# State-space scans: step sizes one operation per slot, no spare decay rows, three taps together, three output pairs on VectorE

## The chip, the core and the metric

The kernel runs on one core of a Trainium2 chip. TensorE (PE), VectorE (DVE), ScalarE (ACT) and GpSimd (POOL) run side by side, each through its own queue in order, and they wait for each other by semaphores; SyncE (SP) issues DMAs. The metric is the time of one execution on the device in microseconds (us), lower is better.

## The reference, cut to what matters

The network has eight blocks on 32 sequences of 113 tokens. The change lies in one of them, the bidirectional state-space block (512 inner channels, 16 states, 4 taps), of which this runs once forward and once on the reversed sequence:

```python
xz = x @ in_w.T
xh, z = jnp.split(xz, 2, axis=-1)
xc = silu(conv_b + sum(xp[:, k:k + L, :] * conv_w[:, k] for k in range(4)))   # xp: xh padded in front
proj = xc @ xproj_w.T                                                        # dt, Bm, Cm
delta = softplus(dt @ dt_w.T + dt_b)
deltaA = exp(delta * A);  deltaBu = (delta * xc) * Bm
h = deltaA * h + deltaBu          # a scan over the tokens, for each of 16 states
y = sum over states of h * Cm;  y = (y + xc * D) * silu(z)
return y @ out_w.T
```

## The kernel before

All tensors keep channels on the 128 partitions; tokens lie along the free axis. The batch is cut into 8 groups of 4 sequences (4 x 113 = 452 columns). A group and a direction make a **half**: 16 halves run in `mamba`, forward and backward in turn, in two calls of `run` of 8 halves each, after a short call that makes the first front. While a half's recurrence runs, the **front** of the half after it (norm, in-projection, convolution, x-projection, step sizes) and the output projection of an earlier one are laid beside it.

The recurrence of a half has 64 **slots**: slot i is state n = i // 4 and channel block j = (0, 2, 1, 3)[i % 4]. In slot i

- ACT computes the decay `dA` = exp(step x A) (`decays`, L1377), into one of two PSUM banks by turns;
- DVE runs the scan (`recur`, L1506) on it and on the input term `dBu`. Blocks 0 and 1 write the state to SBUF (`hs`), blocks 2 and 3 to a PSUM bank (`ssm_ps`); those two DVE multiplies by C itself (`output_term`, L1522);
- POOL makes, once for each state, the output pair of blocks 0 and 1 (`output_terms`, L1462: `hc` = `hs` x C, both in SBUF) and the two input pairs of the next state (`input_terms`, L1451);
- PE adds each `hc` block into the output banks by a product with the identity (`product`, L1286), one slot for each, of the state before.

What else an engine does in a slot stands in its `beside(hf, i)`, by a table of slots at L1137 to L1150: `X_MM` and `Z_MM` (PE in-projections of block m, both into the one bank `XZ`), `TAP` (ACT writes the first tap of the convolution), `CONV` (DVE adds the other three, one in each of the next three slots), `Z_RAW` (ACT copies z out of `XZ`), `SILU` (ACT loads the Silu table, two activations, and loads the Exp table back), `ROWS`, `DT_MM`, `SOFTPLUS` (ACT: Abs, Exp, Ln in one slot), `STEP` (DVE ends the step size). Nothing reorders this: each engine's queue is the order in which the loops write it.

So that the scans can go on while ACT is in a `SILU` slot, ACT computes the decays of the next two slots ahead of it, into `dA_spare` in SBUF (`ahead`, `place`). The scans of these four slots in a half (31, 32, 42, 43) read two SBUF operands, where the others read one from PSUM and one from SBUF.

Of the kernel before, what the change touches and what calls it, by code (L numbers as in the profile page):

```python
# [1117 lines left out]
def mamba(nc, h, c, params):  # L1118
# [18 lines left out]
    MEAN, CENTRE, SQUARE, VAR, RSTD, SCALE = -1, 1, 3, 5, 7, 9  # L1137
    GATE = (2, 3, 5, 6)
    OUT_MM, RES = (8, 11), (10, 13)
    X_MM = [14 + 7 * m for m in range(IB)]  # L1140
    TAP = [16 + 7 * m for m in range(IB)]
    CONV = [15 + 7 * m for m in range(IB)]
    Z_MM = [19 + 7 * m for m in range(IB)]
    Z_RAW = [21 + 7 * m for m in range(IB)]
# [5 lines left out]
    SPARE_ZERO = 50  # L1150

    ahead = {i + 1 + k: 2 + k for i in SILU for k in range(2)}
    place, previous, taken = [], [], {}
    for i in range(SLOTS):
        where = ahead[i] if i in ahead else (i - sum(j < i for j in ahead)) % 2
        place.append(where)
        previous.append(taken.get(where))
        taken[where] = i
    zeroed = {2: -2, 3: -2, place[SLOTS - 2]: -1, place[SLOTS - 1]: 0}
# [3 lines left out]
    with Stage(nc, "ssm_late") as sl, Stage(nc, "ssm") as st:  # L1163
# [93 lines left out]
        def run(parts, weights_late=False):  # L1257
# [8 lines left out]
            with nc.Block(no_gpsimd_drain=True) as block:  # L1266
                @block.sync
                def _(sp):
                    for hf in halves:
# [106 lines left out]
                def _(act):  # L1376
                    def decays(hf, i):  # L1377
                        n, j = i // IB, ORDER[i % IB]
                        if previous[i] is not None:
                            act.wait_ge(s["scan_done"], SLOTS * hf.r + previous[i] + 1)  # L1380
                        elif hf.r:
                            act.wait_ge(s["starts_zero"], 4 * hf.r + zeroed[place[i]])
# [7 lines left out]
                    def beside(hf, i):  # L1390
# [39 lines left out]
                        if hf.front and i in SOFTPLUS:  # L1430
                            m = SOFTPLUS.index(i)
                            at = IB * hf.fronts + m + 1
                            act.wait_ge(s["dt_mm"], at)
# [16 lines left out]
                def _(pool):  # L1450
# [27 lines left out]
                    for k, hf in enumerate(halves):  # L1478
# [3 lines left out]
                        for n in range(S):  # L1482
                            if hf.rec and n:
                                output_terms(hf, n - 1)
# [5 lines left out]
                            if n == S - 3 and hf.front:  # L1490
                                step_input(hf, 0)
                            if n == S - 1:
                                if hf.after:
                                    input_terms(halves[k + 1], 0, 0)
# [1418 lines left out]
```

## Time and profile before

| | us |
|---|---|
| median of 3 runs (lowest, highest) | 6414.39 (6395.42, 6419.84) |
| the profiled execution | 6388.95 |
| its span | 6387.2 |
| of it the 16 halves, about | 1512 to 3341 |

Each number is one profiled execution's. Busy time is of an instruction's own start and end; instructions on DVE overlap by about 0.1 us at their ends, so the step from start to start is what an instruction costs its queue. The idle time of an engine is put down to the instruction that released it.

### The profile page before, as it was taken

Reading aid. Unit: us, or ns where it says so; the run is one execution under the profiler, and the core shown is the slowest. Engines: PE = TensorE matmul, PEld = TensorE weight load, DVE = VectorE, ACT = ScalarE, POOL = GpSimd, SP = SyncE. Lnnn points to the kernel's source line nnn. Section 1 sums busy time; section 2 is a strip of 40 time slices with the busy share of each in tenths; the row PEclk is TensorE's granted clock in tenths of the full one; section 3 lists DMA queues with packets and bytes.
Section 4 is the critical chain, followed back from the end, with each engine's and each line's share of the span. In section 5 each row is a group of like instructions: output and inputs, shape, how many; then the busy total and the mean of one; then the engine's idle time right before and its main releaser. Section 6 shows DMA issues by size and latency. Waiting matters only on the chain. (4 is left out here: it accounts for less than half of the span.)

```text
span 6387.2 us, 65263 instructions
## 1 busy us (share of the span) xinstructions
PE 5081.8 (80%) x21148; PEld 3347.0 (52%) x21148; DVE 3776.1 (59%) x7281; ACT 2136.6 (33%) x3642; POOL 2244.7 (35%) x1326
## 2 busy tenths in 40 slices
PE   7887578856887877877777875976667899999999
PEld 4565346632333333333324443963333798989899
DVE  3665221235898998998984222015553777767775
ACT  1332211104555555555542222224442222222222
POOL 1222030044998998989980000000000221222121
PEclk7666689967899998999998987988877899999999
DMA  1000222321222222222210000640001000000000
GB/s 62 0 0 8 69 84 93 103 68 41 65 68 65 68 65 62 70 63 64 67 56 14 5 0 24 253 178 0 0 0 69 2 4 4 2 4 4 4 4 4
DMA packets 154586, 290.22 MB, mean 45 GB/s; under 512 B 24422, under 2 KB 136082, under 8 KB 145520
## 3 DMA queue, kind: packets, MB, share of 16 engines
q1 hardware_dynamic: 147296, 268.70, 12.6%
q0 software_dynamic: 6144, 14.04, 0.7%
q10 hardware_dynamic: 912, 4.63, 0.2%
q8 instruction: 115, 1.88, 0.1%
q14 instruction: 119, 0.97, 0.1%
HBM read 256.65 MB, written 33.42 MB: 45 GB/s over the span
## 5 line engine op out<-in xcount | busy, mean ns | idle before, releaser
L1297 PE MATMUL ssm_ps<-ssm_hc,net_ident 128*128 128x452 f32 x2048 | 989.2, 610 | 288.6 <-DVE ssm_hc L1529 236.7
L1459 POOL TENSOR_TENSOR ssm_dBu<-ssm_du,ssm_bc 128x904 f32<-128x904 f32 x512 | 1098.9, 2167 | 21.3 <-DMA ssm_bc<-ssm_rows 11.2
L1297 PEld LDWEIGHTS ssm_ps<-ssm_hc,net_ident 128*128 128x128 f32 x2048 | 399.3, 209 | 827.9 <-DVE ssm_hc L1529 414.0
L1386 ACT ACTIVATE ssm_ps<-ssm_step,ssm_decay 128x448 f32<-128x448 f32 x960 | 597.7, 633 | 639.5 <-DVE ssm_ps L1519 406.9
L2724 POOL TENSOR_TENSOR peer_hot_cols<-peer_hot_cols,peer_codesT 128x512 f32<-128x512 f32 (+1 forms) x240 | 285.4, 1189 | 1162.1 <-DVE peer_hot_cols L2740 1162.1
L1519 DVE TENSOR_TENSOR_SCAN ssm_ps<-ssm_ps,ssm_dBu 128x452 f32<-128x452 f32 x480 | 528.9, 1102 | 115.2 <-ACT ssm_ps L1386 56.4
L1468 POOL TENSOR_TENSOR ssm_hc<-ssm_hs,ssm_bc 128x904 f32<-128x904 f32 x256 | 538.9, 2105 | 89.6 <-DVE ssm_hs L1519 89.4
L1519 DVE TENSOR_TENSOR_SCAN ssm_hs<-ssm_ps,ssm_dBu 128x452 f32<-128x452 f32 x480 | 517.3, 1078 | 56.4 <-ACT ssm_ps L1386 32.1
L2634 PE MATMUL peer_ps<-peer_xn,peer_down 128*128 128x226 f32 x2048 | 452.9, 367 | 23.2 <-issue 16.0
L2737 DVE TENSOR_TENSOR peer_hot_rows<-peer_ramp,peer_codesT 128x1024 f32<-128x1024 f32 (+1 forms) x240 | 282.6, 1177 | 284.2 <-PE peer_ps L2649 254.1
L2649 PEld LDWEIGHTS peer_ps<-peer_hot_cols,peer_hot_rows 128*128 128x128 f32 x3616 | 437.8, 193 | 23.8 <-DVE peer_hot_rows L2737 22.4
L2649 PE MATMUL peer_ps<-peer_hot_cols,peer_hot_rows 128*128 128x64 f32 x3616 | 429.1, 273 | 18.5 <-DVE peer_hot_rows L2737 18.5
L2676 PE MATMUL peer_ps<-peer_hid,peer_up 128*128 128x226 f32 x2048 | 399.7, 355 | 1.5 <-DVE peer_hid L2756 1.5
L2634 PEld LDWEIGHTS peer_ps<-peer_xn,peer_down 128*128 128x128 f32 x2048 | 382.9, 195 | 29.2 <-issue 24.1
L2676 PEld LDWEIGHTS peer_ps<-peer_hid,peer_up 128*128 128x128 f32 x2048 | 390.0, 190 | 6.7 <-issue 2.1
L1529 DVE TENSOR_TENSOR ssm_hc<-ssm_ps,ssm_bc 128x452 f32<-128x452 f32 x512 | 307.5, 601 | 0.0
L418 POOL TENSOR_TENSOR at_ex<-at_ex,at_rs 113x452 f32<-113x452 f32 x128 | 125.3, 982 | 447.7 <-DVE at_rs L470 447.7
L2703 ACT ACTIVATE peer_hid<-peer_ps 128x452 f32<-128x452 f32 x256 | 140.0, 547 | 414.7 <-PE peer_ps L2634 414.7
L2696 ACT ACTIVATE peer_weight<-peer_ps 128x512 f32<-128x512 f32 (+1 forms) x240 | 144.3, 609 | 288.3 <-PE peer_ps L2649 288.3
L1072 POOL DMA_INDIRECT sh_got<-slots_out,sh_now_slot x64 | 65.8, 1028 | 457.9 <-DVE sh_now_slot L1095 440.8
L2421 POOL IOTA peer_ramp<- 128x128 f32 x1 | 0.2, 237 | 636.6 <-ACTq L2410 636.6
L2049 POOL MEMSET rw_back<- 128x4520 f32 x1 | 3.9, 3864 | 592.9 <-POOLq L73 592.9
(429 smaller groups left out, 8729.5 us busy)
## 6 DMA issues: line engine op xcount, KB each, us to landing
ssm_bc<-ssm_rows SPq DMA_DIRECT2D x256, 452.0 KB, 3.6
ex_w<-in_l_ffn_w SPq DMA_DIRECT2D x66, 1024.0 KB, 7.7
moe_w_gu<-in_moe_gate_up SPq DMA_DIRECT2D x17, 704.0 KB
slots_in<-rt_zeros SPq DMA_DIRECT2D x17, 640.0 KB, 8.6
xp_rows_in<-slots_in SPq DMA_DIRECT2D x17, 512.0 KB
slots_out<-xp_rows_out SPq DMA_DIRECT2D x16, 512.0 KB
moe_w_dn<-in_moe_down SPq DMA_DIRECT2D x17, 384.0 KB
peer_down<-in_peer_down_t SPq DMA_DIRECT2D x1, 4096.0 KB, 16.5
```

Of the source, the lines that this page charges most:

```text
L1297: nc.tensor.matmul(Y_BANK[j][:, 0:GT], c["ident"][:, :], hc[:, q % 2, j, :], start=False, stop=(n == S - 1))\
L1386: nc.scalar.activation(rows(dA(place[i]))[:, :, lo:lo + N - 1], rows(step[hf.d][:, j, :])[:, :, lo:lo + N - 1], ACT.Exp, scale=decay[hf.d] ...
L1459: nc.gpsimd.tensor_tensor(dBu[:, q % 2, j:j + 2, :], du[hf.d][:, j:j + 2, :], bc[:, q % RING, 0:1, :].to_broadcast([P, 2, GT]), ALU.mult). ...
L1468: nc.gpsimd.tensor_tensor(hc[:, q % 2, 0:2, :], hs[:, q % 2, :, :], bc[:, q % RING, 1:2, :].to_broadcast([P, 2, GT]), ALU.mult).then_inc(s ...
L1519: nc.vector.tensor_tensor_scan(flow(state, hf.d), flow(dA(place[i]), hf.d), flow(dBu[:, q % 2, j, :], hf.d), 0.0, ALU.mult, ALU.add).then_ ...
L1529: nc.vector.tensor_tensor(hc[:, q % 2, j, :], HS_BANK[:, 0:GT], bc[:, q % RING, 1, :], ALU.mult)\
L2634: mm = nc.tensor.matmul(ps[1 + i % 3][:, jj * PT:(jj + 1) * PT], down[:, m, i * J + jj, :], xn[:, m, :], start=(m == 0), stop=(m == DK - 1))
L2649: mm = nc.tensor.matmul(ps[4 + ch % HB][:, t * PB * EB:(t + 1) * PB * EB], hot_rows[:, at % HB, t, :], hot_cols[:, at % HB, t, :], start=T ...
L2676: mm = nc.tensor.matmul(ps[5 + m][:, 0:PT], w_up[:, j, m * P:(m + 1) * P], hid[:, j, :], start=(j == 0), stop=(j == EB - 1))
L2696: nc.scalar.activation(weight[:, :, :, t0:t0 + n], ps[4 + ch % HB][:, 0:n * PB * EB].rearrange("p (t b j) -> p j b t", b=PB, j=EB), ACT.Co ...
L2724: nc.gpsimd.tensor_tensor(hot_cols[:, at % HB, 0:n, :], hot_cols[:, at % HB, 0:n, :], codesT[:, 2, t0:t0 + n].unsqueeze(2).to_broadcast([P ...
L2737: nc.vector.tensor_tensor(hot_rows[:, at % HB, 0:n, :], ramp[:, :].unsqueeze(1).to_broadcast([P, n, P]), codesT[:, 0, t0:t0 + n].unsqueeze ...
```

## The change

Four edits, all in `mamba`, and new slots for nearly everything in `beside`:

1. Abs, Exp and Ln of a step size go to three slots, one each; `STEP` follows at slots 45, 49, 53, 57 (before 50, 54, 58, 62).
2. `dA_spare` goes; every decay uses the two PSUM banks. ACT computes nothing ahead.
3. The three other taps of a block follow each other in the slot of `TAP` on DVE.
4. For states 5, 7 and 8 the output pair is made by DVE (`output_pair`) in slots 26, 35 and 36, not by POOL.

```diff
-    SILU = (30, 41)
-    SOFTPLUS = [48 + 4 * m for m in range(IB)]
-    STEP = [50 + 4 * m for m in range(IB)]
...
+    X_MM = [13 + 6 * m for m in range(IB)]
+    TAP = [15 + 6 * m for m in range(IB)]
+    Z_MM = [16 + 6 * m for m in range(IB)]
+    Z_RAW = [18 + 6 * m for m in range(IB)]
+    SILU = (27, 36)
+    XP_MM, ROWS = 38, 40
+    DT_MM = [42 + 4 * m for m in range(IB)]
+    ABS, EXP, LOG = ([42 + k + 4 * m for m in range(IB)] for k in (1, 2, 3))
+    STEP = [45 + 4 * m for m in range(IB)]
+    DU = {12: 0, 14: 2}
+    PAIR_SLOT = {26: 5, 35: 7, 36: 8}
+    OWN = sorted(PAIR_SLOT.values())
...
+        def pair_wait(eng, q):
+            pool, own = pairs(q)
+            if q % S in OWN:
+                eng.wait_ge(s["hc_own"], own)
+            else:
+                eng.wait_ge(s["hc_pool"], pool)
...
                         if j < 2:
-                            pe.wait_ge(s["hc_pool"], q + 1)
+                            pair_wait(pe, q)
...
-                            if hf.rec and i not in ahead:
+                            if hf.rec:
                                 decays(hf, i)
-                            if hf.rec and i in SILU:
-                                decays(hf, i + 1)
-                                decays(hf, i + 2)
...
+                    def output_pair(hf, n):
+                        q = S * hf.r + n
+                        dve.wait_ge(s["scan_done"], IB * q + AT[1] + 1)
+                        if q >= 2:
+                            dve.wait_ge(s["y_pool"], 2 * (q - 1))
+                        nc.vector.tensor_tensor(hc[:, q % 2, 0:2, :], hs[:, q % 2, :, :],
+                                                bc[:, q % RING, 1:2, :].to_broadcast([P, 2, GT]), ALU.mult).then_inc(s["hc_own"], 1)
...
-                        for m in range(IB):
-                            if CONV[m] < i < CONV[m] + TAPS:
-                                tap(hf, m, i - CONV[m])
+                        if i in TAP:
+                            for t in range(1, TAPS):
+                                tap(hf, TAP.index(i), t)
...
+                                if i in PAIR_SLOT:
+                                    output_pair(hf, PAIR_SLOT[i])
```

The order on ACT around the second `SILU` slot of the second half. L1386 is a decay (L1391 after), L1408 the copy of z (L1413), L1413 and L1418 the two Silu activations (L1418, L1423). Before:

```order
216 L1386 ACTIVATE ssm_ps<-ssm_step,ssm_decay 128x4x112 x4
217 L1386 ACTIVATE ssm_dA_spare<-ssm_step,ssm_decay 128x4x112 x2
218 L1413 ACT_TABLE_LOAD
219 L1413 ACTIVATE ssm_xc<-ssm_conv 128x904
220 L1418 ACTIVATE ssm_z<-ssm_z 128x904
221 L1420 ACT_TABLE_LOAD
222 L1408 ACTIVATE ssm_z<-ssm_ps 128x452
```

After:

```order
272 L1391 ACTIVATE ssm_ps<-ssm_step,ssm_decay 128x4x112 x3
273 L1413 ACTIVATE ssm_z<-ssm_ps 128x452
274 L1418 ACT_TABLE_LOAD
275 L1418 ACTIVATE ssm_xc<-ssm_conv 128x904
276 L1423 ACTIVATE ssm_z<-ssm_z 128x904
277 L1425 ACT_TABLE_LOAD
278 L1391 ACTIVATE ssm_ps<-ssm_step,ssm_decay 128x4x112 x4
```

The two spare decays ahead of the table load are gone, and the copy of the last z block, which stood behind the Silu activations, now stands ahead of them.

The order on PE at the last z projection of a half (L1343 before, L1348 after). L1297 (L1302) are the products with the identity, with the semaphore that each waits for: `ssm_hc_dve` and `ssm_hc_own` are raised by DVE, `ssm_hc_pool` by POOL. Before:

```order
495 L1297 MATMUL ssm_ps<-ssm_hc,net_ident 128x452 [waits ssm_hc_dve] x2
496 L1297 MATMUL ssm_ps<-ssm_hc,net_ident 128x452 [waits ssm_hc_pool] x2
497 L1297 MATMUL ssm_ps<-ssm_hc,net_ident 128x452 [waits ssm_hc_dve]
498 L1343 MATMUL ssm_ps<-ssm_ln_out,ssm_w_in 128x452 [waits ssm_conv_step]
499 L1343 MATMUL ssm_ps<-ssm_ln_out,ssm_w_in 128x452
```

After:

```order
493 L1302 MATMUL ssm_ps<-ssm_hc,net_ident 128x452 [waits ssm_hc_dve] x2
494 L1302 MATMUL ssm_ps<-ssm_hc,net_ident 128x452 [waits ssm_hc_own]
495 L1348 MATMUL ssm_ps<-ssm_ln_out,ssm_w_in 128x452 [waits ssm_conv_step]
496 L1348 MATMUL ssm_ps<-ssm_ln_out,ssm_w_in 128x452
497 L1302 MATMUL ssm_ps<-ssm_hc,net_ident 128x452 [waits ssm_hc_own]
```

The last z projection (slot 34) now stands behind the product of state 7's pair, which DVE makes in its slot 35.

The order on DVE from slot 35 to slot 37 after the change (L1521 a scan, L1531 an output term, L1540 an output pair):

```order
635 L1521 SCALAR_TENSOR_TENSOR ssm_ps<-ssm_ps,ssm_dBu 128x452 [waits ssm_hc_dve,ssm_dA_done,ssm_dbu_done]
636 L1540 TENSOR_TENSOR ssm_hc<-ssm_hs,ssm_bc 128x904 [waits ssm_y_pool,ssm_scan_done]
637 L1521 SCALAR_TENSOR_TENSOR ssm_hs<-ssm_ps,ssm_dBu 128x452 [waits ssm_hc_own,ssm_dA_done,ssm_dbu_done]
638 L1531 TENSOR_TENSOR ssm_hc<-ssm_ps,ssm_bc 128x452 [waits ssm_y_dve,ssm_scan_done,ssm_landed0]
639 L1540 TENSOR_TENSOR ssm_hc<-ssm_hs,ssm_bc 128x904 [waits ssm_y_pool,ssm_scan_done]
640 L1521 SCALAR_TENSOR_TENSOR ssm_ps<-ssm_ps,ssm_dBu 128x452 [waits ssm_hc_dve,ssm_dA_done,ssm_dbu_done]
```

Rows 636 and 639 are new; the others stood there before, without them.

## Rows read from the trace of the kernel before

**Rows 1.** Busy time of each engine in the stretch of the 16 halves.
```profile
1512.00:3341.00 1829.00, 1436.07 (x3184) 607.56 (x3184) 1645.07 (x1945) 969.89 (x1500) 1680.98 (x798) 0.91 0.21 65
```

**Rows 2.** Groups of instructions by line in that stretch.
```profile
L1459 POOL TENSOR_TENSOR ssm_dBu<-ssm_du,ssm_bc 128x904 f32<-128x904 f32 x512 | 1098.9, 2167 | 21.3 <-DMA ssm_bc<-ssm_rows 11.2 <-DVE ssm_ps L1519 7.8 <-DVE ssm_hs L1519 2.4
L1468 POOL TENSOR_TENSOR ssm_hc<-ssm_hs,ssm_bc 128x904 f32<-128x904 f32 x256 | 538.9, 2105 | 89.6 <-DVE ssm_hs L1519 89.4
L1519 DVE TENSOR_TENSOR_SCAN ssm_ps<-ssm_ps,ssm_dBu 128x452 f32<-128x452 f32 x480 | 528.9, 1102 | 115.2 <-ACT ssm_ps L1386 56.4 <-POOL ssm_dBu L1459 28.0
L1519 DVE TENSOR_TENSOR_SCAN ssm_hs<-ssm_ps,ssm_dBu 128x452 f32<-128x452 f32 x480 | 517.3, 1078 | 56.4 <-ACT ssm_ps L1386 32.1 <-POOL ssm_dBu L1459 23.0 <-issue 1.3
L1519 DVE TENSOR_TENSOR_SCAN ssm_ps<-ssm_dA_spare,ssm_dBu 128x452 f32<-128x452 f32 x32 | 109.1, 3408 | 2.2
L1519 DVE TENSOR_TENSOR_SCAN ssm_hs<-ssm_dA_spare,ssm_dBu 128x452 f32<-128x452 f32 x32 | 68.5, 2141 | 0.0
```

**Rows 3.** DVE in order of time, slots 28 to 31 of the fourth half (start, us).
```profile
1907.00 0.60 DVE L1529 TENSOR_TENSOR ssm_hc<-ssm_ps,ssm_bc 128x452 f32<-128x452 f32 x1
1907.73 1.11 DVE L1519 TENSOR_TENSOR_SCAN ssm_ps<-ssm_ps,ssm_dBu 128x452 f32<-128x452 f32 x1
1908.75 1.07 DVE L1519 TENSOR_TENSOR_SCAN ssm_hs<-ssm_ps,ssm_dBu 128x452 f32<-128x452 f32 x1
1909.74 0.60 DVE L1529 TENSOR_TENSOR ssm_hc<-ssm_ps,ssm_bc 128x452 f32<-128x452 f32 x1
1910.26 0.67 DVE L1538 SCALAR_TENSOR_TENSOR ssm_conv<-ssm_ps,ssm_conv_w,ssm_conv 128x448 f32<-128x448 f32 x1
1910.85 2.85 DVE L1519 TENSOR_TENSOR_SCAN ssm_ps<-ssm_dA_spare,ssm_dBu 128x452 f32<-128x452 f32 x1
```

**Rows 4.** The same, of the scan behind a step size (slot 53).
```profile
1952.07 1.11 DVE L1519 TENSOR_TENSOR_SCAN ssm_ps<-ssm_ps,ssm_dBu 128x452 f32<-128x452 f32 x1 [1.07 <-ACT ssm_ps L1386]
```

**Rows 5.** ACT in order of time at that step size.
```profile
1949.59 0.55 ACT L1434 ACTIVATE ssm_ln_square<-ssm_ps 128x452 f32<-128x452 f32 x1 [1.52 <-PE ssm_ps L1359]
...
1950.78 0.67 ACT L1438 ACTIVATE ssm_step<-ssm_ln_square,ssm_one 128x452 f32<-128x452 f32 x1
```

**Rows 6.** ACT at the second Silu slot of that half.
```profile
1930.77 1.28 ACT L1413 ACT_TABLE_LOAD   x1
...
1933.89 1.28 ACT L1420 ACT_TABLE_LOAD   x1
1935.18 0.55 ACT L1408 ACTIVATE ssm_z<-ssm_ps 128x452 f32<-128x452 f32 x1
1935.62 1.19 ACT L1386 ACTIVATE ssm_ps<-ssm_step,ssm_decay 128x448 f32<-128x448 f32 x2
```

**Rows 7.** PE in order of time: a product and a z projection after a wait, another later.
```profile
1917.10 1.88 PE L1297 MATMUL ssm_ps<-ssm_hc,net_ident 128*128 128x452 f32 x2 [5.68 <-DVE ssm_hc L1529]
1918.77 2.41 PE L1343 MATMUL ssm_ps<-ssm_ln_out,ssm_w_in 128*128 128x452 f32 x4
...
1929.55 1.78 PE L1343 MATMUL ssm_ps<-ssm_ln_out,ssm_w_in 128*128 128x452 f32 x4 [1.14 <-DVE ssm_conv L1538]
```

**Rows 8.** DVE in the first front (no POOL work), then beside POOL in a half.
```profile
1442.15 1.10 DVE L142 TENSOR_TENSOR ssm_ln_out<-ssm_ln_centred,ssm_ln_rstd 128x904 f32<-128x904 f32 x1 [5.01 <-ACT ssm_ln_rstd L127]
1447.49 2.11 DVE L1538 SCALAR_TENSOR_TENSOR ssm_conv<-ssm_ps,ssm_conv_w,ssm_conv 128x448 f32<-128x448 f32 x3 [4.24 <-ACT ssm_conv L1401]
...
1875.01 2.72 DVE L142 TENSOR_TENSOR ssm_ln_out<-ssm_ln_centred,ssm_ln_rstd 128x904 f32<-128x904 f32 x1
```

**Rows 9.** POOL in order of time, beside the spare scan shown under it.
```profile
2018.33 4.21 POOL L1459 TENSOR_TENSOR ssm_dBu<-ssm_du,ssm_bc 128x904 f32<-128x904 f32 x2
2022.44 2.14 POOL L1468 TENSOR_TENSOR ssm_hc<-ssm_hs,ssm_bc 128x904 f32<-128x904 f32 x1
2024.49 2.14 POOL L1459 TENSOR_TENSOR ssm_dBu<-ssm_du,ssm_bc 128x904 f32<-128x904 f32 x1
...
2021.59 6.01 DVE L1519 TENSOR_TENSOR_SCAN ssm_ps<-ssm_dA_spare,ssm_dBu 128x452 f32<-128x452 f32 x1
```

More of the change, by code:

```diff
@@ L1135, in mamba @@
     GATES = (2, 3, 0, 1)
[L1137 to L1144, printed above, removed]
-    SILU = (30, 41)
-    XP_MM, ROWS = 44, 45
-    DT_MM = [47 + 4 * m for m in range(IB)]
-    SOFTPLUS = [48 + 4 * m for m in range(IB)]
-    STEP = [50 + 4 * m for m in range(IB)]
[L1150 to L1159, printed above, removed]
+    MEAN, CENTRE, SQUARE, VAR, RSTD, SCALE = -1, 0, 2, 3, 5, 8
+    GATE = (2, 3, 4, 5)
+    OUT_MM, RES = (6, 9), (9, 12)
+    X_MM = [13 + 6 * m for m in range(IB)]
[10 more added lines that the diff above has]
+    OWN = sorted(PAIR_SLOT.values())
     scratch = nc.dram_tensor("ssm_rows", [2, 2, S, GT], F32).ap()
@@ L1200, in dA, with pairs @@
         def dA(k):
-            return A_BANK[k][:, 0:GT] if k < 2 else dA_spare[:, k - 2, :]
+            return A_BANK[k][:, 0:GT]
+        def pairs(q):
+            own = q // S * len(OWN) + sum(n <= q % S for n in OWN)
+            return q + 1 - own, own
+        def pair_wait(eng, q):
[4 more added lines that the diff above has]
+                eng.wait_ge(s["hc_pool"], pool)
         def starts(k, d):
@@ L1242, in _ @@
             def _(dve):
-                for k in range(4):
+                for k in range(2):
                     nc.vector.memset(starts(k, 0), 0.0)
@@ L1378, in decays @@
                         n, j = i // IB, ORDER[i % IB]
[L1379 to L1380 removed]
+                        if i >= 2:
+                            act.wait_ge(s["scan_done"], SLOTS * hf.r + i - 1)
                         elif hf.r:
[L1382 removed]
+                            act.wait_ge(s["starts_zero"], 2 * (hf.r - 1) + i + 1)
                         if n == 0 and hf.fronts:
@@ L1385, in decays @@
                         lo = 1 if hf.d == 0 else 0
-                        nc.scalar.activation(rows(dA(place[i]))[:, :, lo:lo + N - 1],
+                        nc.scalar.activation(rows(dA(i % 2))[:, :, lo:lo + N - 1],
                                              rows(step[hf.d][:, j, :])[:, :, lo:lo + N - 1], ACT.Exp,
@@ L1429, in beside @@
                                 .then_inc(s["row_sent"], 16)
[L1430 to L1433, printed above, removed]
+                        if hf.front and i in ABS:
+                            m = ABS.index(i)
+                            act.wait_ge(s["dt_mm"], IB * hf.fronts + m + 1)
                             nc.scalar.activation(mag[:, m % 2, :], XZ[:, 0:GT], ACT.Abs).then_inc(s["mag_done"], 1)
-                            act.wait_ge(s["mag_done"], at)
+                        if hf.front and i in EXP:
+                            m = EXP.index(i)
+                            act.wait_ge(s["mag_done"], IB * hf.fronts + m + 1)
                             nc.scalar.activation(mag[:, m % 2, :], mag[:, m % 2, :], ACT.Exp, scale=-1.0).then_inc(s["ea_done"], 1)
-                            act.wait_ge(s["ea_done"], at)
+                        if hf.front and i in LOG:
+                            m = LOG.index(i)
+                            act.wait_ge(s["ea_done"], IB * hf.fronts + m + 1)
                             nc.scalar.activation(step[f][:, m, :], mag[:, m % 2, :], ACT.Ln, bias=one[:, 0:1]).then_inc(s["sp_done"], 1)
@@ L1483, in _ @@
                             if hf.rec and n:
-                                output_terms(hf, n - 1)
+                                if n - 1 not in OWN:
+                                    output_terms(hf, n - 1)
                             elif hf.carried is not None:
@@ L1489, in _ @@
                                 input_terms(hf, n + 1, 2)
[L1490 to L1494, printed above, removed]
-                                if hf.front:
-                                    step_input(hf, 2)
-                                if hf.after:
-                                    input_terms(halves[k + 1], 0, 2)
+                            elif hf.after:
+                                input_terms(halves[k + 1], 0, 0)
+                                input_terms(halves[k + 1], 0, 2)
+                            if n in DU and hf.front:
+                                step_input(hf, DU[n])
                         if hf.rec and not hf.after:
```

17 lines of the change are left out of this document (8 added, 9 removed).

## The prediction

> **What bounds the kernel now.** I read the busy times first, then the groups of the stretch in which the halves run, then that stretch in order of time. The halves take 1829 of 6387 us, and nothing outside them is changed. POOL is busy there for 1681 us and DVE for 1645 [rows 1], so either could be the pace. The idle times decide: the scans waited 88.5 us for ACT's decays (56.4 + 32.1) and only 51.0 for POOL's input terms (28.0 + 23.0) [rows 2]. POOL for its part waited 89.4 us for DVE's scans. So DVE's queue is the path, POOL follows close behind it, and a stage costs what DVE executes plus what DVE waits for. A half is about 114 us (1829 / 16).
>
> What one step of DVE's queue costs is read from start to start [rows 3]: a scan 1.0 us (1908.75 to 1909.74), an output term 0.52 before an instruction that doesn't need it and 0.73 before a scan that does (1907.00 to 1907.73), a tap 0.59. A tap or step behind an output term therefore costs only 0.38, since it fills the 0.21 of that wait.
>
> **What goes.** The 64 scans on spare rows took 109.1 + 68.5 = 177.6 us [rows 2]; on PSUM rows they would take 32 x 1.102 + 32 x 1.078 = 69.8. That is 107.8 us less. ACT's three operations of a step size hold it from 1949.59 to 1951.45 in one slot, and the next scan waits 1.07 [rows 4, 5]. With one operation of 0.55 to 0.67 per slot, and about 2.75 us of DVE work between the scan that frees a decay row and the scan that needs it, the decay (0.6) and one such operation fit. I let all of the 88.5 us of waits for ACT go, and count what comes instead below. Together 196 us, or 12.3 for each half.
>
> **What comes, for a half with a front (15 of 16).**
>
> (a) Pair 5, slot 26, with the first Silu slot (27). The pair has 904 elements and reads two SBUF operands. The nearest rows are the norm's last multiply, of the same size and kind: 1.10 alone and 2.72 beside POOL [rows 8]; the longest wait of such an instruction beside POOL is in a scan of 6.01 [rows 9]. I take 2.72 less 0.1 of overlap, since POOL is busy there; less the 0.21 that it fills behind the output term, 2.4. ACT meanwhile needs, from the end of scan 25, a decay (0.6), the first tap of block 2 (0.7), both table loads with the two Silu (1930.77 to 1935.18, 4.4) and a decay (0.6) [rows 5, 6]: 6.3 us. DVE has scan 26, output term, pair, scan 27 and three taps: 1.0 + 0.5 + 2.6 + 1.0 + 2.0 = 7.1. The Silu slot is hidden and only the pair is paid. If the pair took 1.1, DVE would be ready at 5.6, wait to 6.3, and 1.5 would be paid against the 4.8 without pair.
>
> (b) Pair 7, slot 35, and the second Silu slot (36). Here the cover fails. PE's order has the product of pair 7 in its slot 34, ahead of the last z projection. ACT copies that z in slot 36 ahead of its table load, and the decay for slot 37 stands behind the load. So from the end of pair 7 a chain runs through three engines: product and z projection 4.1 us after a PE that has waited (1917.10 to 1921.18) [rows 7], copy 0.55, Silu block 4.4, decay 0.6 [rows 6], in all 9.7. DVE has slot 36 in that time, 1.7 us, and pair 8, which is hidden whatever it costs. It then waits for the rest, and the path is longer by 9.7 - 1.7 = 8.0. With 2.6 for pair 7 itself, 10.6. Behind the waiting scan 37 stand all later scans; POOL has by then made the inputs of state 10 and waits for scan 38, PE waits for both. Before, the z copy stood behind the table load and nothing of this was on the path. Bounds: 7.7 (pair 1.1; z projection 1.8 as in the last of rows 7, product 1.0) to 13.9 (pair as in rows 9).
>
> (c) Three taps in a row take 2.11, 2.03 to the next start, where nothing else runs [rows 8]; they wait for each other. Four blocks: 8.1. Spread out, six taps at 0.38 and six at 0.59 are 5.8. Plus 2.3.
>
> (d) The step's last operation moves from even slots, behind an output term (0.38), to odd ones (0.59): plus 0.8 for four.
>
> (e) ABS waits for a product of PE that now stands right behind a product of a POOL pair. Over the half POOL has a period of three instructions of 2.1 us, 6.3, against 5.5 to 6.0 of DVE, so it falls back until the last of the four comes late. Bounds 0 and 4 x 1.07 [rows 4]; I take 1.0, the last one only. The wait of DVE for POOL at the start of a half stays as it is.
>
> Sum: 2.4 + 10.6 + 2.3 + 0.8 + 1.0 = 17.1 us, times 15 is 257. The last half has no z copy and no front, and pays its three pairs, 7.5. In all 264 against 196: 68 us more. On the profiled execution's own 6389 that is 6457. The median of the runs lies 25 us above it, so I forecast 6414 + 68 = 6482.
>
> The 48 pairs taken from POOL (48 x 2.105 = 101 us [rows 2]) give nothing here, since POOL is hardly waited for. DMAs: the row loads on SP wait for the pair as before, four states ahead. Memsets, semaphores and the norm's new slots move nothing that I can price; the norm's two instructions may gain 0.2 each.
>
> How a DVE instruction waits for POOL is the term with the widest bounds. In rows 9 the scan was issued at 2021.59. POOL's instruction of the moment ended at 2022.54, but the scan ended only at 2027.60, one scan's length after POOL had gone through two more. The Trainium skill (SBUF — State Buffer, "Who interferes with whom") says that the second to issue is blocked until the first finishes; by that rule the scan would have ended near 2023.6, so this row is not what it says. By that rule pair 7, issued some 0.5 before the end of a POOL instruction by my count of the slots, would cost 1.5 and not 2.6, and the time would be 17 us less.
>
> **Rivals.**
>
> One instruction of POOL at most. Pair 7 waits only for the end of the instruction that POOL is in, and costs 1.5. For it: most spare scans took 1.9 to 2.9. Against: 6.01 in rows 9. Time 6482 - 15 x 1.1 = 6465. This is the case that the page named above would give.
>
> The cover almost holds. Pairs cost 1.1, PE runs its products quickly, ABS is never late: 1.5 + 7.7 + 2.3 + 0.8 = 12.3 a half, 185, and 3 for the last half: 188 - 196 = -8, time 6406, no change. For it: POOL, with three pairs fewer, may stand idle when pairs 7 and 8 come. Against: PE will have waited, and after 5.68 us of waiting its products took longer [rows 7].
>
> Faster: POOL is the pace. If POOL's lag is what shapes DVE's waits (through the states' inputs, the pairs that PE waits for, and the port), then taking 101 us from POOL, less 48 x 1.0 in which a pair on DVE keeps it out, shortens the stretch by 53: 6361. It decides if in most halves the scan that ends DVE's wait in slot 37 or at a half's start is released by POOL. Against: POOL is busy for 92% of the stretch and is waited for in 51 us of it.
>
> Starved pairs. Pairs wait through several POOL instructions as the scan in rows 9: pair 7 then costs 3.3 more, pair 5 about 2 (POOL itself runs dry there, since it needs scan 27). 15 x 5.3 = 80 more: 6562.
>
> **How the numbers follow.** Forecast 0.50, with an own range of 6440 to 6525; one instruction at most 0.12; cover almost holds 0.16; faster 0.12; starved 0.10. A change of over 0.5% (32 us) either way can be told from none. Above 6446 lie the forecast but for 0.04, the first rival and the starved one: 0.68. Within: 0.16 and 0.04, less 0.01 of the second rival that lands below: 0.19. Faster: 0.13. The range that leaves out the faster case and half of the starved one is 6400 to 6545.
>
> **What the profile will show.** Right: DVE waits for ACT's decay of about 4 to 6 us once in each front half, behind pair 8; ACT's copy of z just ahead of it waits for PE; PE's product waits for DVE's pair; POOL's idle time in the stretch grows by 150 us or more. Pairs average 2 to 3 us. Waits for ACT behind the step sizes are gone but for the last. Three taps stand 2.0 apart from the next scan. Wrong: if the wait behind pair 8 is under 2 us, or if the pairs average 1.1, or if the scans on PSUM rows become longer, then the sum fails in that term; and the whole fails if the halves stay at 114 us or below.

## The result and the profile after

The changed kernel takes 6549.94 us (median of 4 runs, 6525.87 to 6556.50), the kernel before 6414.55: a ratio of 1.021, 95% interval 1.0176 to 1.0243. The forecast said 6482, in 6400 to 6545. The direction was right; the loss is 135 us, not 68, and lies outside the range. The ratios here and below leave out executions in a slower state of the chip, one of A1's and one of A4's.

The time is in the halves. From the start of the first scan to that of the last it was 1824.3 us and is 1949.5, 125 more. The first front is 5 us longer too (94.8 and 99.3), but C1 and C4 below, whose first fronts are the same, differ by as much (99.4 and 95.1). The profiled execution of the changed kernel also reaches the block 39.5 us later (1459.5, before 1420.0), in stages that the change leaves alone; C1's reached it at 1459.9 and C4's at 1419.3. So times are compared from scan to scan. Busy times of the changed kernel from first to last scan, for [rows 1]:

```profile
1558.75:3508.26 1949.51, 1479.79 (x3180) 612.66 (x3181) 1667.47 (x1957) 965.21 (x1500) 1569.71 (x749) 0.90 0.20 61
```

From first to last scan of the kernel before, DVE was busy for 1643.2 us and GpSimd for 1677.3. DVE is busy 24 us longer in a stretch that grew by 125: it waits. GpSimd has 108 us less work and nothing comes of it. The groups of the changed kernel, for [rows 2], the tap, the output pair and the norm's scaling step with them (busy, mean ns | idle before, and who ended it):

```profile
L1521 DVE TENSOR_TENSOR_SCAN ssm_ps<-ssm_ps,ssm_dBu 128x452 f32<-128x452 f32 x512 | 565.6, 1105 | 176.8 <-ACT ssm_ps L1391 117.9 <-POOL ssm_dBu L1464 6.3 <-DVE ssm_hc L1531 0.4
L1521 DVE TENSOR_TENSOR_SCAN ssm_hs<-ssm_ps,ssm_dBu 128x452 f32<-128x452 f32 x512 | 553.0, 1080 | 78.6 <-ACT ssm_ps L1391 39.7 <-POOL ssm_dBu L1464 36.2
L1549 DVE SCALAR_TENSOR_TENSOR ssm_conv<-ssm_ps,ssm_conv_w,ssm_conv 128x448 f32<-128x448 f32 x180 | 121.2, 674 | 17.1 <-ACT ssm_conv L1406 12.8
L1540 DVE TENSOR_TENSOR ssm_hc<-ssm_hs,ssm_bc 128x904 f32<-128x904 f32 x48 | 91.2, 1901 | 0.0
L142 DVE TENSOR_TENSOR ssm_ln_out<-ssm_ln_centred,ssm_ln_rstd 128x904 f32<-128x904 f32 x7 | 35.7, 5103 | 0.0
L1473 POOL TENSOR_TENSOR ssm_hc<-ssm_hs,ssm_bc 128x904 f32<-128x904 f32 x208 | 436.9, 2101 | 255.1 <-DVE ssm_hs L1521 254.8
```

All scans take 1.1 us now, the long ones are gone. In their place the scans wait 157.6 us for ACT (88.5 before), 115.6 of it in slot 37 alone. That slot in the fourth half, first DVE, then PE, then ACT:

```profile
1991.01 1.52 DVE L1540 TENSOR_TENSOR ssm_hc<-ssm_hs,ssm_bc 128x904 f32<-128x904 f32 x1
...
1994.20 1.25 DVE L1540 TENSOR_TENSOR ssm_hc<-ssm_hs,ssm_bc 128x904 f32<-128x904 f32 x1
2003.21 1.11 DVE L1521 TENSOR_TENSOR_SCAN ssm_ps<-ssm_ps,ssm_dBu 128x452 f32<-128x452 f32 x1 [7.76 <-ACT ssm_ps L1391]
...
1992.59 1.87 PE L1302 MATMUL ssm_ps<-ssm_hc,net_ident 128*128 128x452 f32 x2 [5.98 <-DVE ssm_hc L1540]
1994.26 3.22 PE L1348 MATMUL ssm_ps<-ssm_ln_out,ssm_w_in 128*128 128x452 f32 x4
...
1997.51 0.55 ACT L1413 ACTIVATE ssm_z<-ssm_ps 128x452 f32<-128x452 f32 x1 [7.50 <-PE ssm_ps L1348]
...
2001.19 1.28 ACT L1425 ACT_TABLE_LOAD   x1
2002.49 1.19 ACT L1391 ACTIVATE ssm_ps<-ssm_step,ssm_decay 128x448 f32<-128x448 f32 x2
```

This is the chain of term (b), link by link: pair 7 ends at 1992.53, the product starts, the z projection follows, the copy had waited 7.50, the Silu block runs to 2002.47, then the decay, then the scan.

Two things came out otherwise than in the sum. A second wait follows, in slot 44, behind the first of the four step sizes, 33.3 us over the halves (ACT, then DVE):

```profile
2013.84 0.55 ACT L1438 ACTIVATE ssm_ln_square<-ssm_ps 128x452 f32<-128x452 f32 x1 [3.36 <-PE ssm_ps L1364]
...
2015.00 1.10 DVE L1521 TENSOR_TENSOR_SCAN ssm_hs<-ssm_ps,ssm_dBu 128x452 f32<-128x452 f32 x1 [2.46 <-ACT ssm_ps L1391]
```

And the norm's scaling step takes 5.1 us, not 2.5 (DVE, then POOL):

```profile
1934.16 5.33 DVE L142 TENSOR_TENSOR ssm_ln_out<-ssm_ln_centred,ssm_ln_rstd 128x904 f32<-128x904 f32 x1
...
1932.33 2.11 POOL L1473 TENSOR_TENSOR ssm_hc<-ssm_hs,ssm_bc 128x904 f32<-128x904 f32 x1
1934.38 4.14 POOL L1464 TENSOR_TENSOR ssm_dBu<-ssm_du,ssm_bc 128x904 f32<-128x904 f32 x2
```

By halves (start of a scan 0 to the next, means of six): those without a norm went from 115.3 to 119.1 us, close to the 4.8 forecast for a front half; those with one from 113.3 to 126.7. The miss is in the latter. Of the 9.6 by which the two growths differ, the norm's two instructions on DVE are 4.0; 2.9 are the spare scans, which had been the longer in the halves without a norm, and 2.3 the residual sums' waits for PE.

### The profile page after: what moved, and what is told of

Its sections match the earlier page's. It is cut to its first block and busy times, and to the rows that moved or that the text cites. A ratio compares the mean times of both kernels' runs of the same rounds, so it can differ in the third digit from the quotient of the medians.

```text
span 6554.7 us, 65253 instructions
## 1 busy us (share of the span) xinstructions
PE 5146.0 (79%) x21148; PEld 3360.6 (51%) x21148; DVE 3801.7 (58%) x7295; ACT 2132.4 (33%) x3642; POOL 2137.0 (33%) x1278
## 5 line engine op out<-in xcount | busy, mean ns | idle before, releaser
L1302 PE MATMUL ssm_ps<-ssm_hc,net_ident 128*128 128x452 f32 x2048 | 997.9, 614 | 394.4 <-DVE ssm_hc L1531 194.9
L1302 PEld LDWEIGHTS ssm_ps<-ssm_hc,net_ident 128*128 128x128 f32 x2048 | 393.7, 208 | 963.4 <-DVE ssm_hc L1531 371.5
L1391 ACT ACTIVATE ssm_ps<-ssm_step,ssm_decay 128x448 f32<-128x448 f32 x1024 | 646.9, 635 | 705.6 <-DVE ssm_ps L1521 416.7
L1521 DVE TENSOR_TENSOR_SCAN ssm_ps<-ssm_ps,ssm_dBu 128x452 f32<-128x452 f32 x512 | 565.6, 1105 | 176.8 <-ACT ssm_ps L1391 117.9
L1521 DVE TENSOR_TENSOR_SCAN ssm_hs<-ssm_ps,ssm_dBu 128x452 f32<-128x452 f32 x512 | 553.0, 1080 | 78.6 <-ACT ssm_ps L1391 39.7
L1473 POOL TENSOR_TENSOR ssm_hc<-ssm_hs,ssm_bc 128x904 f32<-128x904 f32 x208 | 436.9, 2101 | 255.1 <-DVE ssm_hs L1521 254.8
L1531 DVE TENSOR_TENSOR ssm_hc<-ssm_ps,ssm_bc 128x452 f32<-128x452 f32 x512 | 308.8, 603 | 0.0
L2752 DVE TENSOR_TENSOR peer_hot_cols<-peer_ramp,peer_codesT 128x512 f32<-128x512 f32 (+1 forms) x240 | 199.9, 833 | 0.0
```

Source lines behind the costliest of these rows:

```text
L1302: nc.tensor.matmul(Y_BANK[j][:, 0:GT], c["ident"][:, :], hc[:, q % 2, j, :], start=False, stop=(n == S - 1))\
L1391: nc.scalar.activation(rows(dA(i % 2))[:, :, lo:lo + N - 1], rows(step[hf.d][:, j, :])[:, :, lo:lo + N - 1], ACT.Exp, scale=decay[hf.d][:, ...
L1473: nc.gpsimd.tensor_tensor(hc[:, q % 2, 0:2, :], hs[:, q % 2, :, :], bc[:, q % RING, 1:2, :].to_broadcast([P, 2, GT]), ALU.mult).then_inc(s ...
L1521: nc.vector.tensor_tensor_scan(flow(state, hf.d), flow(dA(i % 2), hf.d), flow(dBu[:, q % 2, j, :], hf.d), 0.0, ALU.mult, ALU.add).then_inc ...
L1531: nc.vector.tensor_tensor(hc[:, q % 2, j, :], HS_BANK[:, 0:GT], bc[:, q % RING, 1, :], ALU.mult)\
L2752: nc.vector.tensor_tensor(hot_cols[:, at % HB, 0:n, :], ramp[:, 0:PB * EB].unsqueeze(1).to_broadcast([P, n, PB * EB]), codesT[:, 1, t0:t0 ...
```

## The experiments

Each ratio is to the kernel before on the same chip, run beside it. Chips differ (the kernel before took 6383 to 6420 us), so times from different chips are not to be compared directly. "Stretch" is from the first to the last scan start of the profiled execution; the waits are DVE's for ACT, summed over the halves; "scaling" is the busy time of the norm's 7 scaling steps on DVE. A dash is a slot that means something else in that kernel. A1, A4, B2 and B4 also wait in slot 41 (16.0, 32.9, 8.1 and 18.1 us).

| kernel | ratio (95%) | stretch | slot 37 | slot 44 | scaling |
|---|---|---|---|---|---|
| before | 1 | 1824.3 | - | - | 17.5 |
| changed | 1.021 (1.0176 to 1.0243) | 1949.5 | 115.6 | 33.3 | 35.7 |
| A1 z projection ahead | 1.0002 (0.9979 to 1.0025) | 1835.3 | 18.9 | 0 | 32.2 |
| A2 pair 7 on GpSimd | 0.9975 (0.9950 to 1.0001) | 1816.3 | 19.1 | 0 | 36.3 |
| A3 all pairs on GpSimd | 0.9979 (0.9959 to 1.0000) | 1806.7 | 51.1 | 6.3 | 28.3 |
| A4 z copy behind Silu | 1.0061 (1.0026 to 1.0096) | 1863.2 | 0 | 0 | 26.7 |
| A5 step sizes one later | 1.0130 (1.0104 to 1.0156) | 1915.5 | 114.8 | 17.7 | 20.4 |
| B1 scaling in slot 9 | 1.0163 (1.0112 to 1.0215) | 1935.9 | 115.0 | 31.0 | 24.9 |
| B2 A1, norm's slots | 1.0016 (0.9998 to 1.0035) | 1836.7 | 26.6 | 0 | 29.8 |
| B3 A3, A1, norm's slots | 0.9985 (0.9964 to 1.0007) | 1810.6 | 57.3 | 1.7 | 29.4 |
| B4 A1, scaling on GpSimd | 0.9945 (0.9924 to 0.9965) | 1796.5 | 17.3 | 0 | 0 |
| C1 before, steps spread | 0.9966 (0.9949 to 0.9984) | 1803.8 | - | - | 14.2 |
| C2 before, no spare rows | 1.0036 (1.0015 to 1.0057) | 1845.6 | - | - | 18.7 |
| C3 before, taps in a row | 1.0061 (1.0040 to 1.0082) | 1871.0 | - | - | 22.9 |
| C4 C1, out-projections early | 0.9967 (0.9953 to 0.9981) | 1804.5 | - | - | 11.9 |
| C5 C1, scaling on GpSimd | 1.0012 (0.9996 to 1.0028) | 1821.6 | - | - | 0 |
| D1 A3, B1, block 0's taps apart | 1.0019 (0.9999 to 1.0040) | 1831.4 | 51.1 | 2.9 | 26.4 |
| D2 A3, scaling on GpSimd | 0.9918 (0.9893 to 0.9943) | 1772.2 | 51.5 | 9.0 | 0 |
| D3 A2, scaling on GpSimd | 0.9908 (0.9882 to 0.9934) | 1772.8 | 19.6 | 0 | 0 |

(A5's waits in its slots 45 and 49 are given under slot 44.)

**A. The chain of pair 7.**

```diff
-    Z_MM = [16 + 6 * m for m in range(IB)]
+    Z_MM = [16, 22, 28, 33]          # A1
-    PAIR_SLOT = {26: 5, 35: 7, 36: 8}
+    PAIR_SLOT = {26: 5, 36: 8}       # A2
+    PAIR_SLOT = {}                   # A3
-    Z_RAW = [18 + 6 * m for m in range(IB)]
+    Z_RAW = [18, 24, 30, 37]         # A4
```

> The changed kernel with the z projection of block 3 one slot earlier on TensorE (slot 33 and not 34), ahead of the product that waits for VectorE's pair 7. Theory A (order on TensorE: product behind pair 7, z projection, z copy, Silu block, decay): the 7.8 us wait of the scan behind the Silu block falls to 1 to 3 us in each of the 15 halves with a front, 75 to 100 us in all, 6450 to 6475 us. Rival B (the stop of ScalarE's Silu block itself, two table loads and two Silus with only two decay rows, is what is waited for): no more than 30 us, 6520 or above.

> The changed kernel with pair 7 alone back on GpSimd; pairs 5 and 8 stay on VectorE. Theory A (pair 7 starts the chain): the wait of the scan in slot 37 falls from 7.7 to 2 to 4 us, since the product now waits for GpSimd's pair as in the run with all pairs there; 6415 to 6450 us. Rival B (pairs 5 and 8 cost as much as pair 7): 6480 us or more.

> The changed kernel with all 16 pairs of a half on GpSimd, as before the change; everything else of the change stays. Theory A (the pair on VectorE costs its 1.9 us and, by pair 7, the 8.7 us chain): about 91 us of pairs and most of 130 us of chain go, less what GpSimd (48 pairs of 2.1 us more, with 385 us of waiting now) makes VectorE wait: 6380 to 6440 us. Rival B (GpSimd becomes the pace at the Silu blocks, which is why pairs were moved): 6500 us or more, with waits of the scans for dBu. Rival C (two decay rows can't cover the Silu block whatever the pairs do): 6450 to 6500.

> The changed kernel with ScalarE's copy of z block 3 in slot 37, behind the Silu block and its tables (the change has it at the Silu block's own slot 36, ahead of them). The product of pair 7 still stands ahead of the z projection on TensorE. Theory A (it is the copy ahead of the table load that carries TensorE's delay into the Silu block): as with the earlier z projection, 110 to 140 us less than the changed kernel, 6410 to 6440 us. Rival B (the delay of TensorE itself is what costs, through the products and the projection of B, C and dt in slot 38): it comes back as a wait behind slot 40, 6480 us or more.

A1 moves one index by one slot, and takes away the whole loss, more than theory A had for it. The same place in A1 (DVE, PE, ACT):

```profile
1942.57 1.52 DVE L1540 TENSOR_TENSOR ssm_hc<-ssm_hs,ssm_bc 128x904 f32<-128x904 f32 x1
...
1947.48 1.11 DVE L1521 TENSOR_TENSOR_SCAN ssm_ps<-ssm_ps,ssm_dBu 128x452 f32<-128x452 f32 x1 [0.46 <-ACT ssm_ps L1391]
...
1939.95 1.78 PE L1348 MATMUL ssm_ps<-ssm_ln_out,ssm_w_in 128*128 128x452 f32 x4 [1.79 <-DVE ssm_conv L1549]
1944.15 4.06 PE L1302 MATMUL ssm_ps<-ssm_hc,net_ident 128*128 128x452 f32 x10 [2.41 <-DVE ssm_hc L1540]
...
1941.78 0.55 ACT L1413 ACTIVATE ssm_z<-ssm_ps 128x452 f32<-128x452 f32 x1 [0.20 <-PE ssm_ps L1348]
```

The Silu block now runs beside pair 7, the scan and pair 8, and 0.46 us of wait are left in this half. The z projection takes 1.78 us here and not 3.22. The granted clock says why; these are PE's windows over the changed kernel's z projection, its step-size product behind slot 42 and the next one, then over A1's z projection:

```profile
1994.26:1997.27 3.01, 3.01 (x5) 0.50 0.58 156
2011.93:2013.73 1.80, 1.80 (x4) 0.50 0.00 0
2018.98:2019.94 0.96, 0.96 (x4) 1.00 0.26 96
...
1939.95:1941.73 1.78, 1.77 (x4) 1.00 0.00 0
```

In the changed kernel TensorE ran at 0.50 (its 1.2 GHz level) for most or all of that projection in each of the 15 halves, behind waits of 6.0 to 6.4 us. In A1 it was at 1.00 in the half shown, but not everywhere. The same projection two halves before:

```profile
1707.63 3.38 PE L1348 MATMUL ssm_ps<-ssm_ln_out,ssm_w_in 128*128 128x452 f32 x4 [2.21 <-DVE ssm_conv L1549]
```

Behind a wait of 2.21 us it took 1.78 us in four halves of A1, and 3.3 to 3.4 at a clock of 0.50 to 0.54 in seven, so the length of the last wait doesn't tell the level. Even in those seven the scan in slot 37 waits only 1.9 to 2.1 us, where it waited 7.6 to 7.8: most of the gain is the order, and the clock is worth about 1.6 us a half beside it.

The wait in slot 44 went with the other, unasked, in A1, A2 and A4: it was an echo of the same chain, though A1 and A4 have a wait in slot 41 in its place. A2 shows that it takes pair 7: with pairs 5 and 8 left on VectorE the chain is gone. Theory A held in both, and both gained more than it had (the wait in slot 37 is 1.3 us on average in either). A3 is the change without its fourth edit, and with 0.9979 no slower than the kernel before: the whole loss comes with the pairs. Its waits (51 us in slot 37, 40 in slot 28) are those of a Silu block with nothing but scans and taps beside it, which pairs 5 and 8 cover in A2; no rival of GpSimd's pace shows up. In A4 the wait is gone from slot 37, but 32.9 us stand in slot 41, where ACT waits for the projection of B, C and dt behind TensorE's backlog: between its two theories, 20 us above theory A.

```diff
-    DT_MM = [42 + 4 * m for m in range(IB)]
-    ABS, EXP, LOG = ([42 + k + 4 * m for m in range(IB)] for k in (1, 2, 3))
-    STEP = [45 + 4 * m for m in range(IB)]
+    DT_MM = [43 + 4 * m for m in range(IB)]          # A5
+    ABS, EXP, LOG = ([43 + k + 4 * m for m in range(IB)] for k in (1, 2, 3))
+    STEP = [46 + 4 * m for m in range(IB)]
```

> The changed kernel with the step sizes' product, Abs, Exp, Ln and last operation all one slot later (43 to 46 and on); nothing else. Theory A (the product in slot 42 stands behind TensorE's backlog from the chain of pair 7, which is worked off by then for the most part): the wait in slot 44 falls from 2.2 us to about 1 in each half, 15 to 25 us less than the changed kernel, a ratio to the kernel before of 1.017 to 1.019. Rival B (the wait moves along with the product to the next slot): ratio 1.021 as for the changed kernel.

The echo fell from 33.3 to 17.7 us as theory A said. The total fell by more: the stretch by 34 us, the ratio by about 50. In the stretch the scaling step, whose place is unchanged, went from 35.7 to 20.4 us, and the step's last operation stands behind an output term again and costs about 0.3 us instead of 0.5, 12 us in all (term (d) backwards), against 25 us of new waits for GpSimd. The 16 us between stretch and ratio I can't assign.

**B. The halves with a norm.**

```diff
-    MEAN, CENTRE, SQUARE, VAR, RSTD, SCALE = -1, 0, 2, 3, 5, 8
+    MEAN, CENTRE, SQUARE, VAR, RSTD, SCALE = -1, 0, 2, 3, 5, 9   # B1
+    MEAN, CENTRE, SQUARE, VAR, RSTD, SCALE = -1, 1, 3, 4, 5, 9   # B2, B3 (each with A1, B3 with A3)
-                        if hf.norm_in is not None and i == SCALE:
+                        if hf.norm_in is not None and i == SCALE and not hf.rec:                   # B4, C5, D2, D3
...
+                            # on GpSimd, behind state 3's input terms:
+                            if n == 2 and hf.rec and hf.norm_in is not None:
+                                pool.wait_ge(norm.rstd_ready, hf.norms + 1)
+                                nc.gpsimd.tensor_tensor(norm.out[:, :, :], norm.centred[:, :, :],
+                                    norm.rstd[:, :].unsqueeze(1).to_broadcast([P, DK, GT]), ALU.mult).then_inc(norm.ready, 1)
```

> The changed kernel with the norm's scaling step on VectorE back in slot 9 (the change put it in slot 8). Theory A (where this one instruction's request falls against GpSimd's instructions decides whether it takes 2.7 or 5.1 us, and TensorE's second out-projection waits behind it): 3 to 5 us less in each of the 7 halves with a norm, 6515 to 6530 us. Rival B (the whole squeezed row of norm, gate and out-projection costs, not this place): within 10 us of the changed kernel's 6550.

> The changed kernel with the z projection ahead of pair 7 (6415 us in the run of that edit alone) and the norm's steps in slots 1, 3, 4, 5, 9; pairs stay on VectorE. Theory A (the norm's scaling step, 32 us for 7 there, falls to 20 to 27, and the centring step no longer waits 1.5 us each): 10 to 20 us less, 6395 to 6405 us. Rival B (where the scaling step meets GpSimd is chance, as its 2.0 to 6.3 us in that run suggest): within 8 us of 6415.

> The changed kernel with three edits: z projection of block 3 in slot 33, all pairs on GpSimd, and the norm's steps in slots 1, 3, 4, 5, 9 (centre, square, variance, root, scale). Theory A (each of the three terms adds by itself): from 6406 us with the pairs on GpSimd, 25 us less for what is left of the wait in slot 37 (51 us there) and 10 to 20 for the norm: 6360 to 6385 us. Rival B (GpSimd is then the pace and nothing more is to be had): 6395 to 6415 us.

> The changed kernel with the z projection ahead of pair 7 (ratio 1.000 in the run of that edit alone) and the norm's scaling step on GpSimd, behind the input terms of state 3, in the halves that scan. Theory A (the scaling step costs VectorE its 4.6 us on average, in 7 halves): 20 to 32 us less, ratio 0.995 to 0.997. Rival B (the excess of the halves with a norm lies in the gates, residual sums and TensorE's order around it): within 8 us, ratio 0.999 to 1.001. Rival C (GpSimd's 2.1 us more delay the input terms): slower.

> The kernel before with the step sizes spread (ratio 0.9966) and the norm's scaling step on GpSimd in the same place. Its 7 took 14.2 us on VectorE in the run of the spread alone. Theory A: 10 to 14 us less, ratio 0.9945 to 0.995. Rival C (VectorE waits for GpSimd instead): ratio 0.9966 or more.

B1's time is theory A's, but its interval also holds the changed kernel's 1.021, and its stretch fell by 13.6 us, 10.8 of it in the scaling steps: the place counts, for about half of what theory A had. B2 and B3 went to their rivals: the same slot 9, where the step took 2.8 to 3.8 us in B1, gave 3.3 to 4.6 in B2. None of the three arrangements on VectorE made it cheap; the slot alone doesn't decide. B3 also missed on slot 37: 57.3 us stayed, so with the pairs on GpSimd it is the Silu block itself that is waited for and not the z projection. B4 settles the term. On GpSimd the step costs its 2.1 us behind other work:

```profile
L1501 POOL TENSOR_TENSOR ssm_ln_out<-ssm_ln_centred,ssm_ln_rstd 128x904 f32<-128x904 f32 x7 | 14.7, 2104 | 0.0
```

The stretch is 38.8 us shorter than A1's, for 32.2 of scaling steps and 7.9 of the residual sums' waits for PE; the halves with a norm fell from 118.6 to 113.7. In the order before (C5) the same edit made the stretch 18 us longer than C1's. The seven steps' 14 us went, but the scans on spare rows, which also have two SBUF operands beside GpSimd's, grew by 27, and the residual sums' waits by 10. The first group of spare scans, C1, then C5:

```profile
L1522 DVE TENSOR_TENSOR_SCAN ssm_ps<-ssm_dA_spare,ssm_dBu 128x452 f32<-128x452 f32 x32 | 107.8, 3368 | 2.2
...
L1527 DVE TENSOR_TENSOR_SCAN ssm_ps<-ssm_dA_spare,ssm_dBu 128x452 f32<-128x452 f32 x32 | 132.8, 4149 | 2.2
```

C5's ratio is in rival C's range, but the time is in these scans and not in waits for GpSimd, which neither theory had.

**C. Parts of the change alone, in the kernel before.** C1 has the changed kernel's three `if` blocks for Abs, Exp and Ln, in slots 48, 49, 50 and on.

```diff
-    ahead = {i + 1 + k: 2 + k for i in SILU for k in range(2)}
+    ahead = {}                                   # C2 (and the memsets and waits that go with them)
-                            if CONV[m] < i < CONV[m] + TAPS:
-                                tap(hf, m, i - CONV[m])
+                            if i == TAP[m]:      # C3
+                                for t in range(1, TAPS):
+                                    tap(hf, m, t)
-    OUT_MM, RES = (8, 11), (10, 13)
+    OUT_MM, RES = (7, 10), (10, 13)              # C4, with C1
```

> The kernel before with one part of the change alone: each step size's Abs, Exp and Ln in three slots (48, 49, 50 of each four) and not in one. Spare decay rows, taps and pairs as before. Theory A (the waits of VectorE for ScalarE at the softplus are on the path and go, as the changed trace shows): 60 to 90 us less, 6325 to 6355 us. Rival B (the waits come back elsewhere, at the step or for GpSimd's dBu): 6380 to 6415 us.

> The kernel before with one part of the change alone: the spare decay rows are given up, so that all 64 scans of a half run on the two PSUM rows; softplus, taps and pairs as before. The 64 long scans lose 107 us. Theory A (the spare rows covered two Silu blocks of some 5.6 us, and without them the next scan waits 3 us or more behind each, as with all pairs on GpSimd, where it was 1.3 and 1.6 with three taps beside it): the sum comes out near nothing, 6395 to 6440 us. Rival B (the gain of 107 us holds for the most part): 6350 us or less. Rival C (the waits are longer than the long scans were): 6460 or more.

> The kernel before with one part of the change alone: a block's three taps in one slot, in a row (16, 23, 30, 37). Theory A (as forecast, 2.3 us a half from the taps' own duration, plus a wait for ScalarE's first tap in the same slot): 35 to 50 us more, 6455 to 6470 us. Rival B (the later scans on spare rows and their waits for the step sizes absorb part): 6430 us or less.

> The kernel before with the step sizes spread (6397 us in the run of that part alone) and both out-projections one slot earlier on TensorE (7 and 10, not 8 and 11). Theory A (VectorE's residual sums in slots 10 and 13 wait for TensorE, 20 us in all): 8 to 12 us less, 6385 to 6390 us. Rival B (what VectorE no longer waits there it waits for GpSimd at the next half's start): 6395 to 6400 us.

C1 is 22 us faster, in rival B's range and far from theory A's 60: 42 us of waits behind the step sizes go, and 15 come back as waits for GpSimd and 5 as residual sums' waits for PE. C2 is 23 us slower: 107 us of long scans go, and the scans' waits for ACT rise from 88.5 to 209.5, 90 of them in slots 31 and 42 behind the Silu blocks (theory A, 3 us above its range). C3 costs 43 us, theory A by its difference; the chip was a faster one, so its own time is lower than either theory's. C4, on the same chip, gave nothing beyond C1, as rival B had it, though not for its reason: the residual sums wait 6 us less for PE, and the taps 5 us more for ACT.

The fourth edit alone in the kernel before was not run, nor was the new table of slots without the edits.

**D. The best version.**

```diff
-                        if i in TAP:
+                        if i in TAP[1:]:                                   # D1; Z_MM[0] 17, Z_RAW[0] 19
...
+                        if i == TAP[0] + 1: tap(hf, 0, 1); tap(hf, 0, 2)   #     slot 16
+                        if i == TAP[0] + 2: tap(hf, 0, 3)                  #     slot 17
```

> The changed kernel with all pairs on GpSimd (0.2% below the kernel before in its run), the norm's scaling step in slot 9, and the three taps of block 0 moved from slot 15 to slots 16 (two) and 17 (one), its z projection to 17 and its copy to 19. Theory A (of the 2.9 us that slot 15 costs over a bare scan, 0.85 is a wait for ScalarE's first tap and some 0.4 the row itself; both go): 15 to 25 us less than with pairs on GpSimd alone, 0.4 to 0.6% below the kernel before. Rival B (the later z projection and copy delay block 1, whose taps then wait): no more than 0.3% below.

> The changed kernel with all pairs and the norm's scaling step on GpSimd (ratio 0.9979 with the pairs alone; the scaling steps took 28 us on VectorE there). Theory A (the terms add): 20 to 28 us less, ratio 0.9935 to 0.995. Rival C (GpSimd, with 51 more instructions than in the changed kernel, is waited for): 0.997 or more.

> The changed kernel with pair 7 and the norm's scaling step on GpSimd, pairs 5 and 8 on VectorE (ratio 0.9975 with pair 7 alone; the scaling steps took 36 us there). Theory A: 25 to 36 us less, ratio 0.992 to 0.9935. Rival C: 0.997 or more.

D1 went the way of rival B and further: two new waits for ACT of 1.2 us each in slots 16 and 20. D2 and D3 beat both kernels, D3 by 0.9% over the kernel before. Either is somewhat better than theory A; D3's interval (0.9882 to 0.9934) still reaches into its range. Which of the two is the better one their intervals don't tell.

## Why the prediction missed

**What goes** held. Scans fell by 105 us (107.8 forecast), and none of the old waits for ACT is left, though 8.7 us stand in other slots than 37 and 44. It isn't a gain by itself: C1 shows that spreading the step sizes alone is worth 20 us of the 56 that stood behind them.

**(a)** 2.6 against 2.4: slots 26 and 27 take 7.37 us in the half shown, less 2.75 of the bare scans and output term and 2.0 of taps. **(b)** right in its mechanism and its total, 10.4 against 10.6, but the total is partly luck, since two errors cancel. Pair 7 cost 1.65, not 2.6, and here the first rival was right. The chain cost 8.7, not 8.0, since the product and the z projection took 4.9 us, not 4.1, at 0.50 clock. The wait itself is 7.7, where 4 to 6 was expected, since pair 8 took only 1.25 of it. **(c)** the taps as forecast, but a block's taps now stand in the slot of ACT's first tap and wait for it: 12.8 us, 2.6 before. **(d)** as forecast: 0.53 a step, where 0.59 was taken.

**(e)** failed in size, place and cause: 33.3 us against 15, behind the first of the four step sizes and not the last. I looked for the lateness in GpSimd's pairs. It came from (b): PE reached slot 42 late, and its product there ran at 0.50 (1.87 us, against 1.02 for the next three). In the second half it came 1.6 us earlier and ran at 1.00, and nothing was waited for in slot 44.

**The norm's new slots "move nothing that I can price"** is the step that failed outright. [Rows 8] already had the same instruction at 1.10 and at 2.72, and [rows 9] a starved one; I gave that range to the pairs and not to L142, which the change moves too. It cost 18.2 us, and its centring step in slot 0 now waits for PE's mean, 9.4.

Against the sum's 68, then: 18 for (e), 9 for waits for ACT in other slots, 10 for the taps' wait, 18 and 9 for the norm, and 4 for the pairs with the wait in slot 37 (91.2 and 115.6, against 15 x 13.0 and 7.5); less 9 of waits for GpSimd and 4 of residual sums' waits. That comes to 123 of the 125 from first to last scan. These are waits and durations, not distances from start to start, so the match is rough. The rival nearest in time, starved pairs (6562), was not what happened: the pairs averaged 1.90 us, though the last half's pair 5 took 6.59. It was the norm's step that starved. POOL as the pace fell: its idle time before the output pairs rose from 89.6 to 255.1 us.

On the wait of a DVE instruction beside POOL: L142 was issued 0.22 us before POOL's next instruction started and finished only after two more, 1.0 behind the last. The Trainium skill (SBUF — State Buffer, "Who interferes with whom") has the second to issue blocked until the first finishes; these rows, like [rows 9], don't agree, and by it this step would have cost about 1.3 us. In the kernel before all seven of these steps did end 1.0 us behind the end of the POOL instruction that was running when they were issued. In the changed kernel none did: six ended 1.0 behind the next one, and the one shown behind the one after that.

## What to carry to other kernels

In a queue written in slots, what matters of a moved operation is what stands behind it on the engine that waits for it: here one independent projection ahead of the dependent product, instead of behind it, was worth 2% of the kernel (1.021 to 1.0002). Price every instruction whose slot changes that shares a resource with a busy neighbour, also those whose code is untouched. And test one index at a time: three parts of this change alone gave -22, +23 and +43 us, yet together with the new slots and without the pairs (A3) they gave -13, and with the pairs +135.

## What the runs showed of the hardware

- The four-matmul z projection took 3.22 us at a granted clock of 0.50, behind a wait of 6 us, and 1.78 at 1.00. Behind a wait of 2.21 us it was seen at either level (A1: 1.78 us in four halves, 3.3 to 3.4 in seven), and in the changed kernel the clock was at 0.50 again at 2011.93, where PE's last two waits had been 1.24 and 1.71 us.
- A DVE instruction of 904 elements a partition with both operands in SBUF takes 1.10 us alone. Beside GpSimd's stream the same step took 1.2 to 6.4 us in these kernels, and an edit elsewhere changed the sum of seven from 35.7 to 20.4 (A5). On GpSimd it took 2.10 each time.
- All 105 scaling steps that ran on DVE between first and last scan, in the 15 traces that have them, ended 0.95 to 0.96 us behind the end of a GpSimd instruction. For 51 it was the one running when they were issued; in 45 of these GpSimd's next instruction followed at once and took 2.94 to 3.00 us instead of 2.10. For 54 it was one or two instructions later, and always one behind which GpSimd had nothing to start for 2.0 us or more. How long before the end of the running one they were issued doesn't tell the two apart (0.3 to 1.9 us among the 51, 0.1 to 2.1 among the 54). What does was not isolated here. That the port to SBUF is what they meet at is read from who was busy beside them, and from B4.
- Taking a starved instruction off VectorE helped where all scans had a PSUM operand (A1 to B4: 1.0002 to 0.9945) and hurt where spare scans had none (C1 to C5: 0.9966 to 1.0012). The two kernels differ in more than that.
